# The last two images' normalisation, routing and tables inside one step each, the image's root on ScalarE, and another order of the tail, in a vision-transformer kernel with routed experts

## The reference

```python
h = patches @ W.T + b + pos                       # 32 x 1024 x 64
q, k, v = h @ Wq.T + bq, h @ Wk.T + bk, h @ Wv.T + bv
h = layernorm(h + softmax(q @ k.T / 8) @ v @ Wo.T + bo)
logits = h @ gate_w + gate_b                      # 8 experts
idx, prb = argmax(softmax(logits)), its probability
pos = running count of the tokens of that expert, over all images in order
kept = pos < C                                    # C = 1.25 * 32768 / 8
y = (relu(x @ w1[idx] + b1[idx]) @ w2[idx] + b2[idx]) * prb * kept
out = layernorm(h + nan_to_num(y))
```

## Time and profile before

| | us |
|---|---|
| median of 3 runs | 1057.18 (1056.9 to 1058.4) |
| the profiled execution's own time | 1059.39 |
| its span on the core | 1057.6 |
| PE busy | 952.4 (90%) |
| DVE busy | 846.5 (80%) |
| ACT busy | 697.7 (66%) |
| POOL busy | 691.5 (65%) |
| granted TensorE clock, mean | 0.952 |

### The profile page before, as it was taken

The page is one execution under the profiler, slowest core; times in us unless marked ns, Lnnn a source line. Parts: engine busy times, 40 slices in busy tenths (PEclk is TensorE's granted clock), DMA queues, the critical chain, the costliest instruction groups (busy, mean ns, idle before and its releaser), DMA issues.

```text
span 1057.6 us, 19702 instructions
## 1 busy us (share of the span) xinstructions
PE 952.4 (90%) x6046; PEld 530.8 (50%) x6046; DVE 846.5 (80%) x1709; ACT 697.7 (66%) x1192; POOL 691.5 (65%) x689
## 2 busy tenths in 40 slices
PE   3799999999999999999999999999999999856740
PEld 2355545555555555555555555555555555433420
DVE  3667787788888888899989988888889897575561
ACT  2355655777777777777777777777777766545650
POOL 0015444456777777777777777777777777777775
PEclk9699999999999999999999999999999999967775
DMA  3332224334435243334443343424343333035300
GB/s 91 81 77 58 58 59 112 99 85 105 106 79 130 75 110 103 94 96 108 103 107 96 104 109 93 121 68 121 94 104 97 97 93 103 21 106 145 103 22 10
DMA packets 72503, 96.25 MB, mean 91 GB/s; under 512 B 15923, under 2 KB 52230, under 8 KB 72398
## 3 DMA queue, kind: packets, MB, share of 16 engines
q1 hardware_dynamic: 55566, 77.87, 29.7%
q0 software_dynamic: 16832, 17.11, 5.4%
HBM read 43.68 MB, written 18.11 MB: 58 GB/s over the span
## 4 chain that ended last, share of the span: by engine, by line
PE 57%; DVE 23%; ACT 9%; issue 7%; DMA 2%; POOL 1%; SPq 1%; POOLq 0%; DVEq 0%; ACTq 0%
PE p_u L590 14%; DVE mx L1003 8%; PE p_st L568 7%; PE p_misc L605 6%; PE p_misc L513 6%; PE p_misc L669 5%; PE p_misc L536 4%; PE p_sm L550 3%; ACT uu L793 3%; PE p_misc L653 3%; DVE qk L988 2%; ACT qk L759 2%; PE p_st L572 2%; PE p_sm L669 2%; ACT b_h L835 2%
## 5 line engine op out<-in xcount | busy, mean ns | idle before, releaser
L1376 POOL DMA_INDIRECT out<-b_o,b_ix x270 | 295.4, 1094 | 93.4 <-issue 69.3
L1363 POOL DMA_INDIRECT slots<-rows,idx x256 | 252.2, 985 | 146.8 <-issue 87.0
L1003 DVE TENSOR_REDUCE mx<-p_sm 128x1 f32<-128x1024 f32 x252 | 307.1, 1218 | 38.6 <-PE p_sm L552 35.6
L788 ACT ACTIVATE pT<-p_st 128x1024 f32<-128x1024 f32 x256 | 261.8, 1023 | 93.4 <-PE p_st L574 80.5
L590 PE MATMUL p_u<-pT,vv 128*64 128x512 f32 x1024 | 253.7, 605 | 0.0
L568 PE MATMUL p_st<-hi,hx 64*128 64x512 f32 x256 | 127.3, 497 | 5.1 <-ACT pT L788 4.0
L570 PE MATMUL p_st<-hx,hi 64*128 64x512 f32 x256 | 127.3, 497 | 0.0
L590 PEld LDWEIGHTS p_u<-pT,vv 128*64 128x64 f32 x1024 | 61.5, 136 | 105.2 <-issue 94.9
L550 PE MATMUL p_sm<-kh,hi 64*128 64x512 f32 x252 | 103.1, 409 | 10.3 <-DVE mx L1003 6.7
L568 PEld LDWEIGHTS p_st<-hi,hx 64*128 64x128 f32 x256 | 46.9, 183 | 127.3 <-issue 99.7
L835 ACT ACTIVATE b_h<-p_misc,b_w 128x256 f32<-128x256 f32 x244 | 95.6, 475 | 11.5 <-PE p_misc L653 5.2
(11 more groups left out here) (194 smaller groups left out, 1908.5 us busy)
## 6 DMA issues: line engine op xcount, KB each, us to landing
b_w<-in_w SPq DMA_DIRECT2D x136, 193.5 KB
hx<-hi SPq DMA_DIRECT2D x64, 256.0 KB, 3.6
b_in<-slots SPq DMA_DIRECT2D x136, 66.0 KB
lx<-lo SPq DMA_DIRECT2D x32, 256.0 KB
xt<-in_x SPq DMA_DIRECT2D x32, 196.0 KB
out<-b_o,b_ix POOLq DMA_INDIRECT x270
kh<-kh SPq DMA_DIRECT2D x32, 128.0 KB, 2.2
lx<-lo SPq DMA_DIRECT2D x32, 128.0 KB
```

The costliest lines, as they stand in the source:

```text
L788: act.activation(pT[k % 4][:, :], flat(p_st), ACT.Exp).then_inc(exp_done, 1)
L1003: dve.tensor_reduce(mx[:, p, at:at + 1], flat(max_place(n, j)), AX.X, ALU.max).then_inc(max_done, 1)
L1363: pool.indirect_dma_start(slots, bass.IndirectOffsetOnAxis(ap=idx[:, p, j:j + 1], axis=0), rows[:, p, j, :], None, bounds_check=SLOTS - 1, ...
L1376: pool.indirect_dma_start(out_rows, bass.IndirectOffsetOnAxis(ap=b_ix[:, o, j:j + 1], axis=0), b_o[:, o, j, :], None, bounds_check=T - 1, ...
```

## The change

- `norm_root` leaves POOL (two instructions and a wait between) for ACT (Ln, Exp). In steps up to 30 it stands in tile 6 behind `exponent` (tile 5 in steps without a chunk), and `gate_logits` moves on DVE from tile 5 to tile 6, behind `row_max`.
- `LATE` = 30. In steps 31 and 32 DVE runs `late_step`, which takes image b-1 from `attend` through residual, gate, rows, indices and table in one step; `positions` of that image stands in tile 4 or 5 of PE; ACT squares and makes the root in tile 2. POOL scatters image 30 in step 31 behind the store of chunk 23, image 31 in step 32.
- `load_chunk`: rows and weights apart. Chunks in steps: rows first, then each weight load behind a tile of the scores of the step (tiles 4 to 7). Chunks of `rounds`: weights first.
- `rounds` on PE, ACT and DVE finish chunks 25 and 26 ahead of what they begin for chunk 27.
- `HIK` 2 to 1, with the call of `qk_high` moved from the top of the tile's list to its end.

Cut; indentation is reduced:

```diff
@@ -45,8 +45,9 @@
+LATE = NB - 2
 KHK = 1
-HIK = 2
+HIK = 1
@@ -417,22 +416,36 @@
-    if c == 0:
-        sp.wait_ge(free_stored, 16 * (E + 1))
-    for p in range(2):
-        sp.wait_ge(scattered[p], 16 * NT * ((IMAGE[c] + 2 - p) // 2))
-    if c >= NBUF:
-        sp.wait_ge(b_u_ready, c - NBUF + 1)
-        sp.wait_ge(b_ix_ready, c - NBUF + 1)
-        sp.wait_ge(b_yT_ready, c - NBUF + 1)
-    for k in range(2 * PAIRS):
-        v, u = k // 2, k % 2
-        t = slice(v * UT, (v + 1) * UT)
-        sp.dma_start(b_in[:, r, u, t, :], unit_rows(at[k])).then_inc(c_loaded[r], 16)
-        sp.dma_start(b_w[:, r, v, u, :], w[bass.ds(e[k], 1), :, :].rearrange("a k f -> (a k) f"))\
-            .then_inc(c_loaded[r], 16)
+    def rows_in():
+        if c == 0:
+            sp.wait_ge(free_stored, 16 * (E + 1))
+        for p in range(2):
+            sp.wait_ge(scattered[p], 16 * NT * ((IMAGE[c] + 2 - p) // 2))
+        if c >= NBUF:
+            sp.wait_ge(b_u_ready, c - NBUF + 1)
+            sp.wait_ge(b_ix_ready, c - NBUF + 1)
+        for k in range(2 * PAIRS):
+            v, u = k // 2, k % 2
+            sp.dma_start(b_in[:, r, u, v * UT:(v + 1) * UT, :], unit_rows(at[k])).then_inc(c_loaded[r], 16)
+    def weights_in():
+        if c >= NBUF:
+            sp.wait_ge(b_yT_ready, c - NBUF + 1)
+        for k in range(2 * PAIRS):
+            v, u = k // 2, k % 2
+            if c < INSIDE:
+                sp.wait_ge(st_done, NT * (HOST[c] - 1) + NT // 2 + 1 + k)
+            sp.dma_start(b_w[:, r, v, u, :], w[bass.ds(e[k], 1), :, :].rearrange("a k f -> (a k) f"))\
+                .then_inc(c_loaded[r], 16)
+    if c < INSIDE:
+        rows_in()
+        weights_in()
+    else:
+        weights_in()
+        rows_in()
@@ -692,7 +705,7 @@
-    if has(-2):
+    if has(-2) and b < NB:
         positions(b - 2)
@@ -720,6 +733,8 @@
+        if k == 4 and b == NB - 1 or k == 5 and b == NB:
+            positions(b - 1)
@@ -729,12 +744,13 @@
 def rounds():
+    pe.wait_ge(exp_done, NT * NB)
+    turn_back(INSIDE - 1)
     rows_turn(INSIDE)
     for c in range(INSIDE, NC):
...
-        if c == INSIDE:
-            pe.wait_ge(exp_done, NT * NB)
-        turn_back(c - 1)
+        if c > INSIDE:
+            turn_back(c - 1)
@@ -797,10 +813,14 @@
-def last_deviation():
-    act.wait_ge(vs_ready, NB)
-    act.activation(sd[:, :], vs[:, :], ACT.Ln, bias=b_eps[:, 0:1], scale=1.0 / D).then_inc(last_sd_ready, 1)
-    act.wait_ge(last_sd_ready, 1)
+def norm_root(n):
+    act.wait_ge(vs_ready, n + 1)
+    if n >= 1:
+        act.wait_ge(tail_g, GS * (n - 1) + 1)
+        act.wait_ge(pool_step, min(n, LATE))
+        after(act, last_rows_ready, n - LATE)
+    act.activation(sd[:, :], vs[:, :], ACT.Ln, bias=b_eps[:, 0:1], scale=1.0 / D).then_inc(sd_ready, 1)
+    act.wait_ge(sd_ready, n + 1)
     act.activation(rstd[:, :], sd[:, :], ACT.Exp, scale=-0.5).then_inc(rstd_ready, 1)
@@ -879,8 +899,6 @@
-        if k == HIK and has(2):
-            qk_high(b + 2)
@@ -889,36 +907,47 @@
         if has(0):
             exponent(b, k)
+        if k == 2 and LATE < b <= NB:
+            square(b - 1)
+            norm_root(b - 1)
         if m is not None and k == 2:
             xT_copy(m)
-        if k == 5 and b == NB:
-            last_deviation()
+        if k == (5 if m is None else 6) and has(-1) and b <= LATE:
+            norm_root(b - 1)
         if m is not None and k in (4, 5):
             rectify(m, k - 4)
-        if k == 3 and has(-1):
+        if k == 3 and has(-1) and b <= LATE:
             square(b - 1)
-        if k == 7 and has(-1):
+        if k == (7 if b <= LATE else 3 if b < NB else 4) and has(-1):
             gate_exp(b - 1)
         if k in (3, 6) and has(1):
             v_copy(b + 1, q, k // 6)
+        if k == HIK and has(2):
+            qk_high(b + 2)
     if m is not None:
...
 def rounds():
+    deviation(INSIDE - 2)
     rows_beside(INSIDE)
...
     for c in range(INSIDE, NC):
-        deviation(c - 2)
+        if c > INSIDE + 1:
+            deviation(c - 2)
         rectify(c, 0)
+        if c == INSIDE:
+            squares(c - 1)
+            deviation(c - 1)
         if c + 1 < NC:
             rows_beside(c + 1)
...
-        squares(c - 1)
+        if c > INSIDE:
+            squares(c - 1)
     deviation(NC - 2)
     squares(NC - 1)
@@ -1030,17 +1058,18 @@
-def last_residual():
-    dve.wait_ge(t_ready, NB)
-    dve.wait_ge(pool_step, PS * (NB - 1))
-    dve.wait_ge(sq_ready, NB - 1)
-    dve.tensor_tensor(uc[:, :, :], tt[:, :, :], hh[:, (NB - 1) % 2, :, 0:CG], ALU.add)\
+def last_residual(n):
+    dve.wait_ge(t_ready, n + 1)
+    dve.wait_ge(pool_step, PS * LATE)
+    after(dve, last_rows_ready, n - LATE)
+    dve.wait_ge(sq_ready, n)
+    dve.tensor_tensor(uc[:, :, :], tt[:, :, :], hh[:, n % 2, :, 0:CG], ALU.add)\
         .then_inc(uc_ready, 1)
-def last_rows():
-    p = (NB - 1) % 2
...
+def last_rows(n):
+    p = n % 2
+    dve.wait_ge(scattered[p], of_parity(n - 2, p, 16 * NT))
     dve.tensor_tensor(rows[:, p, :, 0:D], uc[:, :, 0:D], per_token(rstd[:, :], D), ALU.mult)
     dve.tensor_scalar(rows[:, p, :, D + 1], rows[:, p, :, D + 1], float(2 * S), None, ALU.add)\
         .then_inc(last_rows_ready, 1)
@@ -1230,6 +1259,36 @@
+def late_step(n, q, back, done):
+    last = n == NB - 1
+    sum_of_squares(done)
+    attend(n, q)
+    last_residual(n)
+    if not last:
+        take_units(n - 2)
+    scaled(done)
+    sum_squares(n)
+    weigh(back)
+    gate_logits(n)
+    gate_gaps(n)
+    gate_choice(n)
+    last_rows(n)
+    finite(back)
+    slot_read(n)
+    probability(n, q)
+    slot_index(n, q)
+    to_numbers(back)
+    residual_sum(back)
+    centre(back)
+    full_units(n)
+    past_experts(n)
+    if last:
+        name_last(n)
+    else:
+        name_units(n)
+        take_units(n)
 def step(b, c, third, has):
@@ -1238,10 +1297,15 @@
-    if has(-2):
+    if b > NB:
+        return
+    if has(-2) and b < NB:
         slot_read(b - 2)
         probability(b - 2, par)
         slot_index(b - 2, par)
+    if b > LATE:
+        late_step(b - 1, q, back, done)
+        return
     for j in range(NT):
@@ -1249,9 +1313,7 @@
             attend(b - 1, q)
-        if j == 1 and b == NB:
-            last_residual()
-        if b - 3 in TABLES[:-1] and j == 1 and b <= NB:
+        if b - 3 in TABLES[:-1] and j == 1:
             take_units(b - 3)
         if b - 2 in TABLES[:-1]:
...
-                if b == NB:
-                    take_units(b - 2)
         if done is not None:
...
-            if j == 5 and b == NB:
-                dve.wait_ge(rstd_ready, NB)
-            if j == 5:
+            if j == (5 if m is None else 6):
                 gate_logits(b - 1)
...
-            if j == 7 and b == NB:
-                last_rows()
         if back is not None:
...
-    if b - 2 == TABLES[-1]:
-        full_units(b - 2)
-        past_experts(b - 2)
-        name_last(b - 2)
 def rounds():
     for c in range(INSIDE - 1, NC):
         sum_of_squares(c - 1)
+        if c <= INSIDE:
+            scaled(c - 1)
...
-        scaled(c - 1)
+        if c > INSIDE:
+            scaled(c - 1)
@@ -1337,28 +1391,22 @@
-def norm_root(n):
-    wait_apart(pool, vs_ready, n + 1)
-    counted(n, 1, pool.tensor_scalar(ve[:, :], vs[:, :], 1.0 / D, EPS, ALU.mult, ALU.add))
-    pool.tensor_tensor(rstd[:, :], ve[:, :], c_half[:, :], ALU.pow).then_inc(rstd_ready, 1)
 def norm_rows(n, p):
     pool.wait_ge(rstd_ready, n + 1)
     if n >= 2:
         pool.wait_ge(scattered[p], of_parity(n - 2, p, 16 * NT))
     pool.tensor_tensor(rows[:, p, :, 0:D], uc[:, :, 0:D], per_token(rstd[:, :], D), ALU.mult)
-    counted(n, 2, pool.tensor_scalar(rows[:, p, :, D + 1], rows[:, p, :, D + 1], float(2 * S), None,
+    counted(n, 1, pool.tensor_scalar(rows[:, p, :, D + 1], rows[:, p, :, D + 1], float(2 * S), None,
...
 def scatter(n, p, tiles):
     if 0 in tiles:
...
-        if n == NB - 1:
-            pool.wait_ge(last_rows_ready, 1)
+        if n >= LATE:
+            pool.wait_ge(last_rows_ready, n - LATE + 1)
         else:
-            wait_apart(pool, pool_step, PS * n + 2)
+            wait_apart(pool, pool_step, PS * n + 1)
     for j in tiles:
@@ -1380,19 +1428,21 @@
 def step(b, c, third, has):
...
+    if b > NB:
+        return
     full = has(0)
-    done = chunk_of(b - 2) if b <= NB else None
+    done = chunk_of(b - 2)
     if done is not None:
-        if b == NB:
-            scatter(b - 2, par, range(NT))
+        if b > LATE:
+            if b < NB:
+                scatter(b - 2, par, range(NT))
             spread_out(done)
+            scatter(b - 1, 1 - par, range(NT))
             return
         scatter(b - 2, par, range(4))
         residual(b - 1, 1 - par)
         scatter(b - 2, par, range(4, NT))
-        norm_root(b - 1)
         spread_out(done, range(5))
         norm_rows(b - 1, 1 - par)
         spread_out(done, range(5, NT))
```

(20 more changed lines are left out.)

## The result

The changed kernel takes 1059.13 us (median of 20 runs, 1057.93 to 1061.96), the kernel before, in the same comparison, 1058.01 (20 runs, 1055.97 to 1059.77): ratio 1.0015, 95% interval 1.0008 to 1.0022. It is 0.15% slower, a little more than the noise, where 12 us less were forecast. The profiled execution has a span of 1057.1 us.

A forecast was written before the change was run, and what follows sets the result against it. PE was taken to bound the steps and POOL's queue of indirect DMAs the tail; 9.6 + 2.5 = 12.1 us off the median 1057.18 gives 1045.1 us, range 1042.5 to 1052.

The forecast's parts named there:

- The stall of max_scores: PE, tile 7: wait behind row_max vanishes once the gate stands behind row_max of tile 6; gain 9.6 us.
- distances 0.23 and 0.33: PE, tile 7: last score pair to row-maximum matmul, then to the chunk's second product; expected 0.23 and 0.33 us.
- the prediction's signs of being wrong: L669 waiting for hh, steps keeping 28.5 on the mean, or stores 28 to 33 later than now less 9.6.
- The root away from POOL: Steps: some 2.4 us a step off POOL, which is not the bound there; gain 0.
- The root on ACT: Tile 6: Ln and Exp fit ACT's pause before v_copy, with 0.2 us of cover on PE; cost 0.
- the rival of the slower side: Tile 6: root overruns ACT's pause, holding v_copy, exponent 7 and PE; 1069 us at 1 us beyond cover; chance 0.05.
- my rivals: Wait only changes place (1054.7, chance 0.10); tail loses (1047.5 to 1052, 0.12); root overfills ACT's pause (0.05).
- The tail: Late steps and rounds: POOL reaches chunk 27 5.8 us earlier, can keep 3.3; gain taken as 2.5 us.
- the pause before chunk 27's store: Tail: POOL, arriving 5.8 us earlier, waits for chunk 27's output, only 0.3 earlier; an expected sign.
- half the clock is gone: Tail: argument that PE's granted clock is 0.71 there and an idle PE doesn't get it back.
- Weight loads spaced: Tiles 4 to 7: last load needed about 9 us after issue, lands in 3.6; cost 0.
- The sum: Whole kernel: 9.6 from the steps plus 2.5 from the tail, 12.1 us, giving a median of 1045.1.

The follow-up runs named there:

- e1: Kernel before with only gate_logits moved to tile 6 in steps with a chunk, root left on POOL: 1058.34 us, ratio 1.0006.
- e2: Changed kernel with POOL's scaling of the rows one store later: 1072.64 us, ratio 1.0136 to the kernel before.
- e3: Changed kernel with POOL's rows one store later and waiting for the gate's last instruction ahead of tile 7: 1044.24 us, ratio 0.9861 to the kernel before.

## Why the prediction was wrong

- **The stall of max_scores, 9.6 us:** its mechanism and its end were right (distances 0.23 and 0.33, no wait for mx). What failed is the sentence "DVE comes from `row_max` at 831.7 and waits for nothing; lg, lb, lm end at 832.4 and ld starts where it does now". In step 28 they take 2.04 us (834.78 to 836.82), not 0.75. I reckoned the instructions at their durations in a place where POOL issued DMAs beside them, and moved them to one where POOL computes. What PE won in tile 7 (0.57 a pair) it lost in the next tile 1 (0.86). (The spare time in an even step is 832.00 less 831.7, 0.3 where it says 0.2; nothing hangs on it.) One of the prediction's signs of being wrong came: the steps kept over 28.5 on the mean (28.6).
- **The root away from POOL, "an engine that is not the bound there: 0":** the second half of the same error. An engine that doesn't bound still sets when its next instruction runs. Rid of the root, POOL's rows moved from tile 7 onto the gate. e1 shows that the gate's own move nearly meets them too. The price on VectorE is 1.31 us in an even step and 0.8 in an odd one, 2.1 a pair. VectorE's idle time took up 1.4 of it (5.6 us a pair before, 4.2 now), and PE pays 0.86 a pair in tile 1, against 0.57 won behind tile 7: the pair got longer by 0.29 counted on PE, by 0.25 counted from `shift` to `shift`.
- **The row that would have warned** was in the trace of before: t_x, 128x8, took 1.31 us beside POOL's residual, and 0.17 in step 32, where no residual ran beside it (VectorE's timeline of the kernel before; its uc is the one at 901.07 of the earlier trace rows). So was lg itself: in steps 2 to 5 of the kernel before, where POOL's rows ran beside it, it took 0.37 to 0.77 us and ended 0.08 behind them. The two rows of t_x:

```profile
901.10 1.31 DVE L1154 TENSOR_TENSOR t_x<-t_m 128x8 f32<-128x8 f32 x1
...
928.70 0.17 DVE L1154 TENSOR_TENSOR t_x<-t_m 128x8 f32<-128x8 f32 x1
```

  The Trainium skill, SBUF — State Buffer, "Who interferes with whom", says that a VectorE instruction with two SBUF inputs contends with a GpSimd instruction that reads SBUF. The traces agree: lg, lb, pri and t_x are held; `row_max`, which reads PSUM, is not, nor was lm (one input, 0.22) beside the rows of one operand. It also says that issue order decides who blocks. Recorded starts don't decide it: pri 0.66 ahead of the rows was held, lg 0.12 ahead in odd steps was not, and POOL's rows kept 1.04 to 1.13 us in e2, e3 and the changed kernel. If POOL is taken to issue when its last wait ends, up to 0.68 us ahead of its record, all these cases agree with the rule; that is an inference. Beside the rows of one operand VectorE paid 0.3 and not their whole length.
- **The root on ACT, 0:** right. Ln and Exp take 0.29 and 0.21 (0.30 and 0.21 in the earlier trace rows), hh ends at 835.19 and `down` starts at 835.53 unheld; the rival of the slower side, that the root doesn't fit, did not come. That the time went up by 1.1 us came from a mechanism that was none of my rivals.
- **The tail, 2.5:** right in size where it was measured alone (2.3 by the runs, 2.4 by the trace). Its steps, in the changed kernel: image 31's scatter begins 45.8 us behind `shift` 31 instead of 51.2, 5.4 earlier (5.8 forecast); the pause before chunk 27's store is there, 2.92 us. The changed kernel's own 4.2 behind `shift` 31 is larger because that `shift` was itself late. (The words "half the clock is gone" overstate their row: 0.71 is the mean of stretches at 0.50 and at 1.00.)
- **Weight loads spaced, 0:** not settled; on the other chips they are worth 6 to 15 us, which says nothing sure of the first.
- **The sum:** e3 has all parts and no hold on the gate (t_x is still held 1.31 in odd steps, as before): 1044.24, ratio 0.9861, which is 1042.5 by the forecast's base of 1057.2, against 1045.1. Its trace, of its slowest execution (1048.81), bears out both terms: `shift` 31 is 8.2 earlier than before (884.30), although the first step took 1.9 longer there (as in e1's trace), for the 9.6; and the last store is 154.1 behind it instead of 156.75, 2.6 for the 2.5. So the sum was right for a kernel without the collision, and e3 isn't the kernel that was forecast.

## What to carry to other kernels

Before an instruction is moved, look at what the engine that shares its path to SBUF does at the new place, and where that engine goes when work is taken off it: two right forecasts of a stall removed and an engine relieved can meet in one collision. The sign in a profile is one instruction form with two durations; list its mean by place, not over the kernel. Where two engines are both released by the same semaphore, a wait that lets the short list of the bound engine pass first can be worth more than the move itself (28.4 us between e2 and e3).

## What the runs showed that I had not expected

- A VectorE instruction of 0.22 us on 128x64 takes as much as 1.53 to 1.83 beside a POOL instruction of 1.07, longer than the other's whole record. Where POOL had nothing left to wait for, the hold starts some 0.68 us ahead of the recorded start of its instruction; it ends 0.1 behind its end. Two executions of a step that differ by 0.03 us in that distance differ by 1.5 us in length.
- The same rows with one SBUF operand take POOL 1.57 us instead of 1.06 and lengthen VectorE's instruction by 0.3 only.
- On three chips PE's semaphore updates came microseconds behind the recorded ends of its matmuls, and VectorE and ScalarE stood still with it, in all kernels that ran there, 1.07 to 1.09 times the usual time for the kernel before and over 1.2 for the others; the cause is open.
